# Second layer's experts on one core: row tiles in five buffers in place of three

## The chip, the core and the metric

The kernel runs on one core of a Trainium2 chip. The core has a matrix engine (TensorE; PE in the profile, with its weight loads as PEld), a vector engine (DVE), a scalar engine (ACT), GpSimd (POOL) and a queue engine (SyncE; SP). Sixteen DMA engines move data between the chip's memory and the core's; SP issues most transfers (queue q1), and POOL issues the indirect ones (queue q0). The metric is the device time of one execution in microseconds. Before the change it is 3275.32 us, the median of three runs (3271.12 to 3281.46).

## The reference, cut to what matters

The program is a network of two layers on x of 16 x 512 rows of 256 numbers: a local attention with a feed-forward part, a small routed expert part, a linear attention, and at last a mixture of 8 experts over all 8192 rows, two experts a row. The change touches only this last part:

```python
h = gelu(einsum('ecd,edf->ecf', padded_x, w1), approximate=False)   # D 256 -> F 512
out_padded = einsum('ecf,efd->ecd', h, w2)                          # F 512 -> D 256
out_rep = where(valid[:, None], out_padded[gather_idx], 0.0)
out_w = out_rep * w_topk.reshape(-1)[:, None]
src = src + out_w.reshape(T, TOP_K, D).sum(axis=1)
x = x + gate * rmsnorm(src, norm2_w)
```

## The kernel before, in words

`experts_block` is the last stage of the program. The stage before it has written each row to a list in DRAM (`padded`), sorted by expert; a row there is 260 numbers, the 256 of the row and four more (its destination, and what its weight is made of). The list is cut into 71 tiles (NTILEX) of 256 rows. A tile belongs to one expert, and tile i goes through these steps.

SP loads the rows into `xe` (`load_rows`, L3905 to 3908, 260 KB), and the expert's matrices into `w1` and `w2` (`load_up`, `load_down`, 512 KB each). All three have WB = 3 buffers, and tile i uses buffer i % 3. Destination and expert are numbers that SP reads from a list (`number`, a TENSOR_LOAD of its own for each).

PE transposes the rows (`transpose`, L4116), DVE copies them to `xT` (L4021), PE multiplies with w1 (`up`, L4128), ACT applies gelu (L4011), PE multiplies with w2 (`down`, L4140), and DVE scales the result with the row's weight into `ye` (`copy_out`, L4046). Before that DVE takes destination and weight out of the four extra numbers of the row (`place_rows`, L4030 to 4040). Its first instruction (L4030) waits until the rows sent from the same buffer three tiles ago have arrived.

POOL sends the results with two indirect transfers a tile that add 128 rows each to `src_rows` in DRAM (L3994). Rows of two tiles can have one destination, so the two sends of a tile wait until those of the tile before have arrived. With `ye` and `place` there are three buffers too.

PE's order is transpose(i+2), up(i+1), down(i). DVE's is copy_rows(i+2), place_rows(i), copy_out(i). So place_rows(i) stands behind the transpose of tile i+2, and ahead of copy_out(i) and copy_rows(i+3). In SP's loop step i the rows of tile i+3 are loaded first, once place_rows(i) is over (`weight_ready`), then w1 once up(i) is over, then w2 once down(i) is over. Between them, once in four tiles, stand a load of a gate row, from step 12 on a load of 512 rows of `src_rows` that are complete (L3931), and from step 18 on two stores of the output (L3941). These 512 rows are normalized by DVE and added by POOL (L3982).

After the last tile the last 512 rows are loaded, normalized and stored.

Of the kernel before, what the change touches and what calls it, by code (L numbers as in the profile page):

```python
# [10 lines left out]
ALU = mybir.AluOpType  # L11
AX = mybir.AxisListType

P = 128
D = 256
# [33 lines left out]
ROWS_X = 256  # L49
NTILEX = T * TOPK // ROWS_X + E - 1  # L50

ROW = D + 4
# [3786 lines left out]
def experts_block(nc, m, I, mods_dram, src_dram, padded_dram, out):  # L3839
# [5 lines left out]

    RT = ROWS_X // P
    WB = 3
    ctx = ExitStack()
    with nc.cleanup_on_exit(), ctx:
        def sem(name):  # L3850
# [2 lines left out]
        sb = tile_maker(nc, ctx)  # L3853
        w1 = sb("w1_x", [P, WB, C, F1])
        w2 = sb("w2_x", [P, WB, NF1, D])
        xe = sb("xe", [P, WB, RT, ROW])
        xT = sb("xT_x", [P, 2, C, ROWS_X])
        actT = sb("actT_x", [P, 2, NF1, ROWS_X])
        ye = sb("ye", [P, WB, RT, D])
# [39 lines left out]
        @block.sync  # L3899
        def _(sp):  # L3900
            def number(at, top):
                return nc.values_load(m.tile_x[0:1, at:at + 1], engines=[mybir.EngineType.SP], min_val=0, max_val=top,
                                      skip_runtime_bounds_check_because="the list is clamped to the experts and rows")

            def load_rows(i):  # L3905
                r = number(NTILEX + i, E * CAP)
                sp.dma_start(xe[:, i % WB, :, :], padded_dram[bass.ds(r, ROWS_X), :].rearrange("(t p) d -> p t d", p=P))\
                    .then_inc(x_in[i % WB], 16)

            def load_up(i, e):  # L3910
                sp.dma_start(w1[:, i % WB, :, :], I["L1_ffn_w1"][bass.ds(e, 1), :, :]
                             .rearrange("e (c p) f -> p (e c) f", p=P)).then_inc(w1_in[i % WB], 16)

            def load_down(i, e):
                sp.dma_start(w2[:, i % WB, :, :], I["L1_ffn_w2"][bass.ds(e, 1), :, :]
                             .rearrange("e (f p) d -> p (e f) d", p=P)).then_inc(w2_in[i % WB], 16)

            def rows_sent(n):
                for u in range(WB):
                    sp.wait_ge(sent[u], 16 * RT * ((n + WB - 1 - u) // WB))  # L3920

            def load_gate(b):
                if b:
                    sp.wait_ge(gates_ready, b)
                sp.dma_start(gate_norm[:, b, :], mods_dram[1, b, 2, :].partition_broadcast(P)).then_inc(gates_in, 16)

            def load_src(b):
                rows_sent(complete(b))
                if b >= 2:
                    sp.wait_ge(x_ready, 2 * (b - 1))  # L3930
                sp.dma_start(src[:, b % 2, :, :], src_dram[b * S:(b + 1) * S, :].rearrange("(t p) d -> p t d", p=P))\  # L3931
                    .then_inc(src_in[b % 2], 16)

            def load_last(b, h):
                sp.dma_start(src[:, b % 2, 2 * h:2 * h + 2, :],  # L3935
                             src_dram[b * S + h * (2 * P):b * S + (h + 1) * (2 * P), :].rearrange("(t p) d -> p t d", p=P))\
                    .then_inc(src_in[h], 16)

            def store(b, h):
                sp.wait_ge(x_ready, 2 * b + h + 1)  # L3940
                sp.dma_start(out[b, h * (2 * P):(h + 1) * (2 * P), :].rearrange("(t p) d -> p t d", p=P),  # L3941
                             x_half(b, h).rearrange("p (t d) -> p t d", t=2)).then_inc(stored, 16)

            for i in range(WB):
                load_rows(i)
                e = number(i, E - 1)
                load_up(i, e)
                load_down(i, e)
            sp.dma_start(n2w[:, :], I["L1_ffn_norm2_w"].partition_broadcast(P)).then_inc(gates_in, 16)
            for i in range(NTILEX):  # L3950
                if i + WB < NTILEX:
                    e = number(i + WB, E - 1)
                    sp.wait_ge(xT_done, i + 1)
                    sp.wait_ge(weight_ready, 4 * i + 4)
                    load_rows(i + WB)
                    sp.wait_ge(up_done, 2 * i + 2)
                    load_up(i + WB, e)
                    sp.wait_ge(y_done, i + 1)
                    load_down(i + WB, e)
                if i % 4 == 0:  # L3960
                    if i // 4 < B:
                        load_gate(i // 4)
                    if i >= 12:
                        load_src((i - 12) // 4)
                if i % 4 == 2 and i >= 18:
                    store((i - 18) // 4, 0)
                    store((i - 18) // 4, 1)
            rows_sent(NTILEX)
            sp.wait_ge(x_ready, 2 * (B - 2))  # L3969
            for h in range(2):  # L3970
                load_last(B - 1, h)
            for h in range(2):
                store(B - 2, h)
            for h in range(2):
                store(B - 1, h)
            sp.wait_ge(stored, 16 * 2 * B)
# [38 lines left out]
        def _(dve):  # L4015
# [8 lines left out]
            def place_rows(i):  # L4024
                u = i % WB
                dve.wait_ge(x_in[u], 16 * (i // WB) + 16)

                if i >= WB:
                    dve.wait_ge(sent[u], 16 * RT * (i // WB))
                dve.tensor_copy(place[:, u, :], xe[:, u, :, D]).then_inc(place_ready, 1)  # L4030

                dve.wait_ge(weight_ready, 4 * i)
                dve.scalar_tensor_tensor(out=second[:, :], in0=xe[:, u, :, D + 1], scalar=m.row_x[:, i:i + 1],
                                         in1=m.own[:, :], op0=ALU.subtract, op1=ALU.not_equal).then_inc(weight_ready, 1)
                dve.tensor_tensor(change[:, :], xe[:, u, :, D + 3], xe[:, u, :, D + 2], ALU.subtract)\
                    .then_inc(weight_ready, 1)
                dve.wait_ge(weight_ready, 4 * i + 2)
                dve.tensor_tensor(change[:, :], change[:, :], second[:, :], ALU.mult).then_inc(weight_ready, 1)
                dve.wait_ge(weight_ready, 4 * i + 3)
                dve.tensor_tensor(weight[:, u, :], change[:, :], xe[:, u, :, D + 2], ALU.add).then_inc(weight_ready, 1)  # L4040

            def copy_out(i):
                dve.wait_ge(y_done, i + 1)
# [64 lines left out]
        @block.tensor  # L4108
        def _(pe):
            def transpose(i):  # L4110
                pe.wait_ge(x_in[i % WB], 16 * (i // WB) + 16)
                if i >= 2:
                    pe.wait_ge(xT_ready, i - 1)
                for t in range(RT):
                    for c in range(C):
                        mm = pe.transpose(bank(m, 6 + i % 2)[:, c * ROWS_X + t * P:c * ROWS_X + (t + 1) * P],  # L4116
                                          xe[:, i % WB, t, c * P:(c + 1) * P], m.ident[:, :])
                mm.then_inc(xT_done, 1)

            def up(i):  # L4120
                pe.wait_ge(xT_ready, i + 1)
                pe.wait_ge(w1_in[i % WB], 16 * (i // WB) + 16)
                for h in range(2):
                    if i >= 2:
                        pe.wait_ge(gelu_ready, 2 * (i - 2) + h + 1)
                    for f in (2 * h, 2 * h + 1):
                        for c in range(C):
                            mm = pe.matmul(bank(m, 2 * (i % 2) + h)[:, (f % 2) * ROWS_X:(f % 2 + 1) * ROWS_X],  # L4128
                                           w1[:, i % WB, c, f * P:(f + 1) * P], xT[:, i % 2, c, :],
                                           start=(c == 0), stop=(c == C - 1))  # L4130
                    mm.then_inc(up_done, 1)

            def down(i):
                pe.wait_ge(gelu_ready, 2 * i + 2)
                pe.wait_ge(w2_in[i % WB], 16 * (i // WB) + 16)
                if i >= 2:
                    pe.wait_ge(ye_ready, i - 1)
                for t in range(RT):
                    for f in range(NF1):
                        mm = pe.matmul(bank(m, 4 + i % 2)[:, t * D:(t + 1) * D], actT[:, i % 2, f, t * P:(t + 1) * P],  # L4140
                                       w2[:, i % WB, f, :], start=(f == 0), stop=(f == NF1 - 1))
                mm.then_inc(y_done, 1)

            transpose(0)
            transpose(1)
            up(0)
            for i in range(NTILEX):
                if i + 2 < NTILEX:
                    transpose(i + 2)
                if i + 1 < NTILEX:  # L4150
                    up(i + 1)
                down(i)
# [50 lines left out]
```

## Time and profile before

| | |
|---|---|
| Time before, median of 3 runs | 3275.32 us |
| Profiled execution, its own time | 3295.55 us |
| Span of the profiled execution | 3293.8 us |
| PE busy in the span | 3056.6 us, 93% |
| Last stage | from about 2692 us to the end |
| Transposes of the first and last tile start | 2695.03 and 3251.28 us |

The profiled execution is 20 us longer than the median of the three runs, 0.6%. Durations are read from it, and differences are taken over to the median as they are. Times in the rows are microseconds from the span's start. A busy PE is not a PE at its peak, since matmuls are pipelined and their ends are modelled.

### The profile page before, as it was taken

How to read it: one execution, taken by the hardware profiler on the slowest of the kernel's cores; microseconds unless marked ns; L12 is line 12 of the kernel's file. 1: busy time of each engine (PE TensorE's matmuls, PEld its weight loads, DVE VectorE, ACT ScalarE, POOL GpSimd, SP SyncE). 2: the span in 40 equal slices, each digit the busy share in tenths (PEclk: the TensorE clock that was granted, in tenths of full speed). 3: DMA queues.
4: the chain of work that ended last, by engine and by line, in shares of the span. 5: the costliest groups of instructions: out<-in, count | busy, mean ns of one | idle time of the engine just before them, and what ended most of it. 6: DMA issues, size and time to landing. Idle time of an engine off the chain costs nothing. (4 is left out here: it accounts for less than half of the span.)

```text
span 3293.8 us, 55752 instructions
## 1 busy us (share of the span) xinstructions
PE 3056.6 (93%) x18230; PEld 1911.0 (58%) x18230; DVE 2188.0 (66%) x6629; ACT 1590.7 (48%) x3518; POOL 1202.1 (36%) x1522
## 2 busy tenths in 40 slices
PE   7899999999998995899999999999998859998897
PEld 3566767767765663344444444444443338887786
DVE  7777777777772224778888888888887732445455
ACT  3556565555551113476666666666665521111111
POOL 2123232232244113234444444444443234444445
PEclk9999999999999998899999999999999979999998
DMA  8110010010113971212222222222222128888885
GB/s 271 5 49 25 24 48 24 25 47 24 48 61 116 319 243 44 65 56 74 75 75 75 75 75 75 75 75 75 75 75 72 46 93 218 223 235 222 213 228 148
DMA packets 269343, 337.23 MB, mean 102 GB/s; under 512 B 43951, under 2 KB 218658, under 8 KB 269104
## 3 DMA queue, kind: packets, MB, share of 16 engines
q1 hardware_dynamic: 240112, 296.62, 29.4%
q0 software_dynamic: 28464, 34.71, 4.8%
q10 hardware_dynamic: 544, 3.15, 0.2%
q8 instruction: 113, 1.85, 0.2%
q14 instruction: 110, 0.90, 0.1%
HBM read 225.77 MB, written 113.95 MB: 103 GB/s over the span
## 5 line engine op out<-in xcount | busy, mean ns | idle before, releaser
L2827 DVE TENSOR_REDUCE negmax<-psum 128x1 f32<-128x512 f32 x1024 | 667.0, 683 | 164.6 <-PE psum L3380 149.2
L2445 ACT ACTIVATE pT<-psum 128x512 f32<-128x512 f32 x1024 | 576.0, 595 | 294.2 <-PE psum L3409 200.7
L3380 PE MATMUL psum<-k_stack,q_stack 96*128 96x512 bf16 x1024 | 358.6, 389 | 21.1 <-DVE negmax L2827 16.7
L3409 PE MATMUL psum<-q_stack,k_stack 99*128 99x512 bf16 x1024 | 361.1, 384 | 18.1 <-ACT pT L2445 10.5
L3994 POOL DMA_INDIRECT src_rows<-ye,place x142 | 223.3, 1573 | 330.8 <-DVE place L4030 126.0
L940 ACT ACTIVATE probs<-probs,negmax 128x256 f32<-128x256 f32 x512 | 252.8, 495 | 137.6 <-DVE negmax L1032 133.8
L4011 ACT ACTIVATE actT_x<-psum 128x512 f32<-128x512 f32 x142 | 84.8, 597 | 485.2 <-PE psum L4128 478.5
L3423 PE MATMUL psum<-pT,v_tile 128*32 128x512 f32 x2048 | 269.1, 609 | 1.0 <-ACT pT L2445 1.0
L4128 PE MATMUL psum<-xT_x,w_x 128*128 128x256 f32 x1136 | 263.6, 386 | 0.0
L4140 PE MATMUL psum<-w_x,actT_x 128*128 128x256 f32 x1136 | 256.6, 379 | 0.0
L1032 DVE CUSTOM_DVE_ANT_0 probs<-psum,band_mask 128x256 f32<-128x256 f32 x512 | 181.4, 420 | 104.6 <-PE psum L1296 104.1
L849 POOL TENSOR_TENSOR x<-x,scaled 128x256 f32 (+1 forms) x64 | 46.7, 729 | 552.7 <-DVE scaled L1094 552.7
L4140 PEld LDWEIGHTS psum<-w_x,actT_x 128*128 128x128 f32 x1136 | 215.9, 190 | 29.3
L1354 PE MATMUL psum<-w,actT 128*128 128x256 f32 x1024 | 231.5, 379 | 1.3 <-ACT actT L958 0.8
L4128 PEld LDWEIGHTS psum<-xT_x,w_x 128*128 128x128 f32 x1136 | 215.3, 195 | 27.7
L1348 PE MATMUL psum<-x2T,w 128*128 128x512 f32 x512 | 226.3, 595 | 1.0 <-DVE x2T L1084 1.0
L3380 PEld LDWEIGHTS psum<-k_stack,q_stack 96*128 96x128 bf16 x1024 | 97.3, 98 | 210.6 <-DVE negmax L2827 127.6
L3409 PEld LDWEIGHTS psum<-q_stack,k_stack 99*128 99x128 bf16 x1024 | 99.3, 98 | 201.5 <-ACT pT L2445 109.1
L1354 PEld LDWEIGHTS psum<-w,actT 128*128 128x128 f32 x1024 | 193.4, 190 | 33.7 <-issue 6.2
L4046 DVE TENSOR_SCALAR ye<-psum,weight 128x256 f32<-128x256 f32 x142 | 62.0, 478 | 183.4 <-PE psum L4140 183.0
L1348 PEld LDWEIGHTS psum<-x2T,w 128*128 128x128 f32 x512 | 97.8, 191 | 111.2 <-issue 108.5
L2258 POOL DMA_INDIRECT padded<-src,scatter_idx x128 | 125.6, 981 | 91.3 <-DVE scatter_idx L2973 54.7
(400 smaller groups left out, 5708.9 us busy)
## 6 DMA issues: line engine op xcount, KB each, us to landing
w_x<-in_L_ffn_w_dram SPq DMA_DIRECT2D x142, 512.0 KB, 4.4
w_e<-in_L_ffn_w_dram SPq DMA_DIRECT2D x46, 1024.0 KB, 7.4
q_stacks<-q_part SPq DMA_DIRECT2D x192, 128.0 KB
q_stack<-q_stacks SPq DMA_DIRECT2D x64, 384.0 KB, 4.4
padded<-w_e SPq DMA_DIRECT2D x32, 650.0 KB, 6.1
xe<-padded SPq DMA_DIRECT2D x71, 260.0 KB
gate_rows<-mods SPq DMA_DIRECT2D x66, 256.0 KB, 3.5
x<-in_L_attn_x_dram SPq DMA_DIRECT2D x16, 512.0 KB, 8.7
```

Source lines behind the costliest of these rows:

```text
L940: ins = act.activation(probs[:, h, :], probs[:, h, :], ACT.Exp, bias=negmax[:, h:h + 1], scale=-1.0, accum_out=zsum[:, t % 2, h:h + 1])
L1032: ins = dve.tensor_tensor_reduce(probs[:, h, :], bank(m, j)[:, i * 2 * P:(i + 1) * 2 * P], m.band_mask[:, variant, :], scale=-1.0, scalar= ...
L1348: mm = pe.matmul(bank(m, at), m.w1_0[:, c, f * P:(f + 1) * P], x2T[:, c, :], start=(c == 0), stop=(c == C - 1))
L1354: mm = pe.matmul(bank(m, at)[:, 0:D], actT[:, f, t * P:(t + 1) * P], m.w2_0[:, f, :], start=(f == 0), stop=(f == NF0 - 1))
L2445: act.activation(pT[:, 4 * (s % 2) + r, :], bank(m, 2 + n % 2), ACT.Exp, scale=float(DHQ) ** -0.5)\
L2827: dve.tensor_reduce(negmax[:, p // REP, h:h + 1], bank(m, max_bank(b, 16 * g + p)), AX.X, ALU.max, negate=True).then_inc(max_read, 1)
L3380: pe.matmul(bank(m, max_bank(b, 16 * g + p)), q_stack[0:K_SCORE, h, t * P:(t + 1) * P], k_stack[0:K_SCORE, g, :], start=True, stop=True).t ...
L3409: pe.matmul(bank(m, 2 + n % 2), k_stack[:, g, kc * P:(kc + 1) * P], q_stack[:, REP * g + r, :], start=True, stop=True).then_inc(sT_done, 1)
L3423: mm = pe.matmul(bank(m, VB)[VW * r:VW * (r + 1), :], v_tile[:, par, kc, g, :], pT[:, 4 * (s % 2) + r, :], start=(kc == 0), stop=(kc == NT ...
L3994: pool.indirect_dma_start(src_dram, bass.IndirectOffsetOnAxis(ap=place[:, i % WB, t:t + 1], axis=0), ye[:, i % WB, t, :], None, bounds_che ...
L4128: mm = pe.matmul(bank(m, 2 * (i % 2) + h)[:, (f % 2) * ROWS_X:(f % 2 + 1) * ROWS_X], w1[:, i % WB, c, f * P:(f + 1) * P], xT[:, i % 2, c, ...
L4140: mm = pe.matmul(bank(m, 4 + i % 2)[:, t * D:(t + 1) * D], actT[:, i % 2, f, t * P:(t + 1) * P], w2[:, i % WB, f, :], start=(f == 0), stop ...
```

## The change

The row tiles `xe` get XB = 5 buffers; tile i is in buffer i % 5 everywhere it is read or written. The weights, `ye`, `place` and the semaphores of the loads keep three. The first extra load (tile 3) is issued ahead of the loop, once tile 0 has been transposed. In loop step i SP now loads the rows of tile i+4 in place of those of tile i+3. For that it waits until tile i+1 has been transposed and until place_rows(i-1) is over; before it waited, for tile i+3, until place_rows(i) was over. The load of tile i+4 thus stands one step earlier in SP's order, and what it waits for in DVE's order is two tiles earlier. The loads of w1 and w2 are unchanged, but no wait for place_rows(i) stands ahead of them any more.

```diff
     WB = 3
+    XB = 5
...
-        xe = sb("xe", [P, WB, RT, ROW])
+        xe = sb("xe", [P, XB, RT, ROW])
...
-                sp.dma_start(xe[:, i % WB, :, :], padded_dram[bass.ds(r, ROWS_X), :].rearrange("(t p) d -> p t d", p=P))\
+                sp.dma_start(xe[:, i % XB, :, :], padded_dram[bass.ds(r, ROWS_X), :].rearrange("(t p) d -> p t d", p=P))\
...
             sp.dma_start(n2w[:, :], I["L1_ffn_norm2_w"].partition_broadcast(P)).then_inc(gates_in, 16)
+            sp.wait_ge(xT_done, 1)
+            load_rows(WB)
             for i in range(NTILEX):
+                if i + WB + 1 < NTILEX:
+                    sp.wait_ge(xT_done, i + 2)
+                    if i:
+                        sp.wait_ge(weight_ready, 4 * i)
+                    load_rows(i + WB + 1)
                 if i + WB < NTILEX:
                     e = number(i + WB, E - 1)
-                    sp.wait_ge(xT_done, i + 1)
-                    sp.wait_ge(weight_ready, 4 * i + 4)
-                    load_rows(i + WB)
                     sp.wait_ge(up_done, 2 * i + 2)
                     load_up(i + WB, e)
...
-                dve.tensor_copy(place[:, u, :], xe[:, u, :, D]).then_inc(place_ready, 1)
+                dve.tensor_copy(place[:, u, :], xe[:, i % XB, :, D]).then_inc(place_ready, 1)
```

Three more instructions of place_rows and the transposes get the same new buffer number.

SP's order in the last stage, before, from the last load ahead of the loop to step 1. TENSOR_LOAD reads a number, the DMA on xe loads rows, those on w_x load w1 (128x2x512) and w2 (128x4x256):

```order
L3949 DMA n2w_rows<-in_L_ffn_norm_w_dram 128x256
L3902 TENSOR_LOAD tile_x
L3902 TENSOR_LOAD tile_x [waits d_weight_ready,d_xT_done]
L3907 ISA
L3907 DMA xe<-padded 128x2x260
L3911 ISA [waits d_up_done]
L3911 DMA w_x<-in_L_ffn_w_dram 128x2x512
L3915 DMA w_x<-in_L_ffn_w_dram 128x4x256 [waits d_y_done]
L3925 DMA gate_norm<-mods 128x256
```

The same place after:

```order
L3950 DMA n2w_rows<-in_L_ffn_norm_w_dram 128x256
L3903 TENSOR_LOAD tile_x [waits d_xT_done]
L3908 ISA
L3908 DMA xe<-padded 128x2x260
L3903 TENSOR_LOAD tile_x [waits d_xT_done]
L3908 ISA
L3908 DMA xe<-padded 128x2x260
L3903 TENSOR_LOAD tile_x
L3912 ISA [waits d_up_done]
L3912 DMA w_x<-in_L_ffn_w_dram 128x2x512
L3916 DMA w_x<-in_L_ffn_w_dram 128x4x256 [waits d_y_done]
L3926 DMA gate_norm<-mods 128x256
```

Two row tiles (3 and 4) now stand ahead of the loop's first w1, where there was one, and only transposes hold them. The number of the expert is read behind the rows' load, not ahead of its wait. In later steps the one load of rows in a step is that of a tile further on. The order on PE, DVE, ACT and POOL is the same as before.

## Rows read from the trace of the kernel before

**Rows 1.** Waits in 2692:3294: engine, line, releaser: us in total, times, longest.

```profile
POOL src_rows L3994 <- DMA src_rows<-ye,place: 64.7, 17, 6.4
...
PE psum L4116 <- DMA xe<-padded: 50.6, 25, 12.6
...
DVE place L4030 <- DMA src_rows<-ye,place: 34.8, 24, 5.8
```

**Rows 2.** Waits of the SP queue in 2692:3294.

```profile
SPq L3954 <- DVE weight L4040: 127.7, 53, 8.6
```

**Rows 3.** Transposes of tile 2 and tile 70: start, us, engine, line.

```profile
2706.21 0.60 PE L4116 MATMUL psum<-ident,xe 128*128 128x128 f32 x4
...
3251.28 0.60 PE L4116 MATMUL psum<-ident,xe 128*128 128x128 f32 x4
```

**Rows 4.** Timeline of an early tile, 2750 to 2760.

```profile
2750.29 0.60 PE L4116 MATMUL psum<-ident,xe 128*128 128x128 f32 x4
...
2751.88 0.16 DVE L4030 CAST place<-xe 128x2 uint32<-128x2 f32 x1
...
2753.14 0.37 SPq L3907 DMA_DIRECT2D xe<-padded  x1
...
2757.64 0.60 PE L4116 MATMUL psum<-ident,xe 128*128 128x128 f32 x4
...
2757.84 0.88 DVE L4046 TENSOR_SCALAR ye<-psum,weight 128x256 f32<-128x256 f32 x2 [4.87 <-PE psum L4140]
...
2758.63 0.68 DVE L4021 COPY xT_x<-psum 128x512 f32<-128x512 f32 x1
```

**Rows 5.** Timeline of a late stretch, 3052 to 3080.

```profile
3061.69 1.55 POOL L3994 DMA_INDIRECT src_rows<-ye,place  x1 [0.30 <-issue]
...
3070.41 0.17 DVE L4030 CAST place<-xe 128x2 uint32<-128x2 f32 x1 [5.77 <-DMA src_rows<-ye,place]
...
3071.16 1.55 POOL L3994 DMA_INDIRECT src_rows<-ye,place  x1 [7.91 <-DVE place L4030]
3071.68 0.38 SPq L3907 DMA_DIRECT2D xe<-padded  x1
...
3076.26 1.11 PE L4116 MATMUL psum<-ident,xe 128*128 128x128 f32 x4 [5.44 <-DMA xe<-padded]
```

**Rows 6.** First sends of tiles 1, 11, 31, 62, 67 and 70, POOL's timeline.

```profile
2723.59 1.55 POOL L3994 DMA_INDIRECT src_rows<-ye,place  x1 [4.61 <-PE psum L4128]
...
2796.60 1.55 POOL L3994 DMA_INDIRECT src_rows<-ye,place  x1 [3.70 <-DVE place L4030]
...
2966.30 1.55 POOL L3994 DMA_INDIRECT src_rows<-ye,place  x1 [4.91 <-DVE place L4030]
...
3224.08 1.55 POOL L3994 DMA_INDIRECT src_rows<-ye,place  x1 [4.06 <-DVE place L4030]
...
3257.24 1.55 POOL L3994 DMA_INDIRECT src_rows<-ye,place  x1 [1.99 <-DMA src_rows<-ye,place]
...
3275.50 1.55 POOL L3994 DMA_INDIRECT src_rows<-ye,place  x1 [3.02 <-DMA src_rows<-ye,place]
```

**Rows 7.** Sends (L3994) in 2715:2800, then 2900:3224, then 3224:3294.

```profile
DMA to landing us min/median/max: 4.6/4.9/5.8
...
DMA to landing us min/median/max: 4.1/5.9/8.6
...
DMA to landing us min/median/max: 2.7/3.6/4.9
```

**Rows 8.** Busy time in two stretches, with granted clock, DMA share, GB/s.

```profile
2715.00:2800.00 85.00, 85.00 (x418) 74.83 (x417) 24.59 (x97) 14.33 (x24) 37.17 (x24) 1.00 0.89 219
...
2900.00:3224.00 324.00, 294.41 (x1405) 253.15 (x1404) 162.73 (x577) 46.57 (x78) 145.27 (x95) 0.98 0.84 223
```

**Rows 9.** Scaling of tile 31's result, DVE's timeline.

```profile
2953.78 0.88 DVE L4046 TENSOR_SCALAR ye<-psum,weight 128x256 f32<-128x256 f32 x2 [3.57 <-PE psum L4140]
```

**Rows 10.** PE's waits in 2800:2900, columns as in rows 1.

```profile
PE psum L4116 <- DMA xe<-padded: 5.1, 4, 2.6
```

More of the change, by code:

```diff
@@ L4029, in place_rows @@
                     dve.wait_ge(sent[u], 16 * RT * (i // WB))
-                dve.tensor_copy(place[:, u, :], xe[:, u, :, D]).then_inc(place_ready, 1)
+                dve.tensor_copy(place[:, u, :], xe[:, i % XB, :, D]).then_inc(place_ready, 1)
                 dve.wait_ge(weight_ready, 4 * i)
-                dve.scalar_tensor_tensor(out=second[:, :], in0=xe[:, u, :, D + 1], scalar=m.row_x[:, i:i + 1],
+                dve.scalar_tensor_tensor(out=second[:, :], in0=xe[:, i % XB, :, D + 1], scalar=m.row_x[:, i:i + 1],
                                          in1=m.own[:, :], op0=ALU.subtract, op1=ALU.not_equal).then_inc(weight_ready, 1)
-                dve.tensor_tensor(change[:, :], xe[:, u, :, D + 3], xe[:, u, :, D + 2], ALU.subtract)\
+                dve.tensor_tensor(change[:, :], xe[:, i % XB, :, D + 3], xe[:, i % XB, :, D + 2], ALU.subtract)\
                     .then_inc(weight_ready, 1)
@@ L4039, in place_rows @@
                 dve.wait_ge(weight_ready, 4 * i + 3)
-                dve.tensor_tensor(weight[:, u, :], change[:, :], xe[:, u, :, D + 2], ALU.add).then_inc(weight_ready, 1)
+                dve.tensor_tensor(weight[:, u, :], change[:, :], xe[:, i % XB, :, D + 2], ALU.add).then_inc(weight_ready, 1)
             def copy_out(i):
@@ L4116, in transpose @@
                         mm = pe.transpose(bank(m, 6 + i % 2)[:, c * ROWS_X + t * P:c * ROWS_X + (t + 1) * P],
-                                          xe[:, i % WB, t, c * P:(c + 1) * P], m.ident[:, :])
+                                          xe[:, i % XB, t, c * P:(c + 1) * P], m.ident[:, :])
                 mm.then_inc(xT_done, 1)
```

## The prediction, made before the changed kernel ran

> **What bounds the kernel now.** I read the page first: PE is busy for 93% of the span, so the last stage looks bound by PE too. Then, since the change touches that stage alone, I read the waits from 2692 us to the end, and here the reader is to see that PE waits for one thing only, the rows `xe`: 50.6 us in 25 waits [rows 1]. Two of the 25, 12.6 us for the first tile (the longest) and 3.4 us for the second, are the start of the stage and no part of this. That leaves 34.6 us in 23 waits. The transposes of tiles 2 and 70 start 545.1 us apart, 8.02 us a tile over 68 tiles [rows 3]; undisturbed tiles take 7.35 us [rows 4]. So PE loses 68 x 7.35 = 499.8 against 545.1, 45.3 us, of which 34.6 are waits and some 11 what comes with them (after a wait of 5.44 us four transposes took 1.11 us in place of 0.60 [rows 4, 5]; the granted clock is 0.98 in the late stretch and 1.00 in the early one [rows 8]). 45 us is what a PE that never waits would give back, if nobody else were in the way.
>
> The next view was the SP queue's own waits: it stands 127.7 us in 53 waits ahead of the load of rows, for place_rows [rows 2]. In the early stretch that is harmless. The load leaves 2753.14 and the tile is transposed from 2757.64, 4.5 us later, with no wait [rows 4]. In the late stretch the timeline shows what holds it. place_rows is held up 5.77 us by a send of three tiles ago, until 3070.41; the rows' load leaves 1.27 us behind it, and PE stands until 3076.26 [rows 5]. So the root of PE's wait is the sends. In the waits they stand three more times, with 64.7 us before POOL's next send and 34.8 us before place_rows in 24 waits [rows 1].
>
> Last I followed the sends by themselves, since each pair waits for the landing of the pair before. One cycle is the first send, the second 1.85 us behind it (1.55 and a pause of 0.30 [rows 5]), its landing, and 0.75 us from there to the next first send (3070.41, where the landing also frees place_rows, to 3071.16 [rows 5]). With the median landing of 5.9 us from 2900 to 3224 [rows 7] this makes 1.85 + 5.9 + 0.75 = 8.5 us. Measured, tiles 31 to 62 are (3224.08 - 2966.30) / 31 = 8.32 us apart [rows 6]. In the early stretch it is 1.85 + 4.9 + 0.75 = 7.5 by the medians [rows 7] and (2796.60 - 2723.59) / 10 = 7.30 measured [rows 6], just PE's 7.35. After the last loads it is (3275.50 - 3257.24) / 3 = 6.09 us [rows 6], with landings of 3.6 us [rows 7]. The lag shows who drives. Tile 31's result is being scaled at 2953.78 [rows 9] and is sent at 2966.30 [rows 6], 12.5 us later. The very last pair still starts on a landing, at 3275.50 [rows 6]. So from about tile 24 to the end a chain of sends at 8.3 us a tile sets the pace, and PE's waits for rows are how PE is told to slow down.
>
> **The change part by part.**
>
> The rows' lead. A load issued at 2753.14 for a tile due at 2757.64 is now issued one step of SP earlier, without place_rows(i) ahead: one tile (7.35) and up to the 2.6 us by which it stood behind the end of down, so 12 to 14 us of lead where there were 4.5 [rows 4]. Late, place_rows(i-1) has to be over; even a wait of 5.77 us there [rows 5] leaves more than 4.5 us. PE's 23 waits for rows go: at most -45.3 us for PE. What is late next is place_rows itself, which also stands ahead of copy_out(i) and of the copy for up(i+3) in DVE's order. Undisturbed it starts 1.6 us behind the transpose of tile i+2, and up(i+3) follows the transpose of tile i+4, 14.7 us behind it. After place_rows come its small operations (no more than the 1.26 us from 2751.88 to SP's issue), scaling and copy (0.88 + 0.68, in 1.47 us) [rows 4]. So place_rows may be late by 14.7 - 1.6 - 1.26 - 1.47 = 10.4 us before PE stops, where now 5.77 stop it. PE can be some 5 to 10 us further ahead, about one tile. After that it is again held at the sends' 8.3 us a tile.
>
> What PE's extra tile is worth. The chain of sends does not start earlier for it, as its results wait 12.5 us already [rows 6, 9]. It pays at the end alone: with PE and its loads one tile further ahead, the loads end one tile earlier for the sends, and one to two more tiles are sent at 6.09 in place of 8.32 us: 1.3 x 2.23 = -3 us. Before tile 24, where the chain is caught up with PE, I take another -3 us for PE's first waits, 5.1 us in four, up to 2900 us [rows 10]; its bounds are 0 and -5.
>
> The loads' place in time. The loads of rows and w1 no longer follow a landing by 1.3 us [rows 5] but come at the end of down, next to w2. No row shows sends beside loads in this order. From below: the early stretch has 0.89 of the DMA engines busy and landings of 4.9 us, the late one 0.84 and 5.9 [rows 7, 8], so more load need not mean later landings, and at the early 7.30 us the 31 tiles from 31 to 62 would be 31 x 1.02 = -32 us. From above: landings up to 8.6 us occur [rows 7], and PE runs ahead for some 20 tiles first, with its loads at 7.35 in place of 8.0 us a tile; 0.6 us more on each landing there is +12. I take +2, near the late stretch's rows, which have the full traffic.
>
> The extra row load ahead of the loop, and the two row tiles before the first w1: 260 KB each, with 4.5 us and more until used, beside PE's first transposes; 0, at most +0.5. SP's second number read now stands between rows and w1; w1 has three tiles of lead, 0. The two more buffers cost nothing in time. The end (load, norm and stores after 3277) is unchanged.
>
> Sum against the profiled execution's own 3295.55: -3 - 3 + 2 = -4, so 3291.5; it stands 20 us over the median, so the same difference on 3275.3 gives 3271.
>
> Where a rule would have it otherwise: sends that are issued amid loads land after 5.9 us (median), without them after 3.6 [rows 7], so the loads cost the sends 2.3 us. The Trainium skill, "DMA: Bandwidth & Descriptors", Queues, rings and completion order, says that each DMA engine goes round robin between the queues that have work. By that a send would wait for its share of packets alone, whatever stands behind the load's first ones, and shifting the loads would cost or give nothing: the +2 would be 0, the forecast 3269. The spread from 4.1 to 8.6 us in one stretch [rows 7] speaks against so even a share, and I keep both ends.
>
> **The rivals.**
>
> *The sends follow PE (3230).* If landings only suffer because loads are released by a landing and hit the next pair at once [rows 5], loads spread in time let the chain run at the early 7.30 us, and all of PE's 45 us are won: 3275.3 - 45 = 3230. For it: 7.30 us was held at 0.89 of the DMA engines [rows 6, 8]. Against it: late tiles also load `src_rows` and store, so 7.35 us a tile would need 223 x 8.32 / 7.35 = 252 GB/s where no stretch here has over 223 [rows 8].
>
> *Half of it (3255).* The chain goes at 7.8 in place of 8.32 us over some 38 tiles: -20.
>
> *Slower (3287).* PE, freed, runs its loads ahead at 7.35 us a tile from tile 16 to about tile 36, until place_rows is 10 us late. The sends of these 20 tiles land 0.6 us later each, +12, and are not paid back, as the later pace is the landings' as well. It decides from about 0.5 us a landing on. For it: landings rose from 4.9 to 5.9 with the extra traffic [rows 7]. Against it: the bytes are the same, and what is loaded early isn't loaded late.
>
> *The change doesn't do what it says:* PE still waits for rows, since its lead is eaten by the queue. 12 us of lead against 4.5 speaks against it; the time would be the 3275 of before, within the forecast's range.
>
> **How the numbers follow.** Forecast (the sends keep the pace) 0.54, with its own range 3262 to 3281; half 0.17; all 0.12; slower 0.17. A measurement of this kernel tells about 0.3%, 9.8 us, from no change: faster is under 3265.5, slower over 3285.1. Faster: 0.12 + 0.16 + 0.03 of the forecast's = 0.31; slower: 0.14 + 0.02 = 0.16; within: 0.53. The range leaves out the case at 3230 and half of the slower one, 0.12 + 0.08: 3246 to 3287.
>
> **What would show it.** Right: PE's waits for `xe` fall to the 16 us of the start, and PE waits instead ahead of up (L4128) for the copy to `xT`, or ahead of down for `ye`; place_rows' waits for sends grow well past 34.8 us, single ones to some 10; the lag of sends behind scaling grows from 12.5 to about 20 us; the sends of tiles 31 to 62 stay at 8.2 to 8.5 us. Wrong: sends of the late stretch at 7.3 to 7.8 us (the two faster cases) or landings over 6.5 us in the median (slower), and a lag that does not grow.

## The result

The changed kernel takes 3294.15 us, the median of 5 runs (3293.78 to 3299.34), where before takes 3275.7 (3271.12 to 3281.7): the ratio is 1.0055, with a 95% interval from 1.0039 to 1.007. It is slower by 18 us, outside the forecast range and on the side to which I had given 0.16. Run again later on another chip it was 1.0048 (1.003 to 1.0066).

The profiled execution of the changed kernel took 3294.15 us, span 3292.4. The profiled execution of before, from which all rows ahead of the prediction come, took 3295.55. So the two profiled executions show no loss, where the timed runs show 18 us, and this is the first thing to explain.

What the prediction said of the waits came out. These are the waits of the last stage after, in 2692:3294, columns as in [rows 1]:

```profile
DVE place L4035 <- DMA src_rows<-ye,place: 149.6, 39, 5.8
...
PE psum L4133 <- DVE xT_x L4026: 23.8, 10, 3.5
...
POOL src_rows L3999 <- DMA src_rows<-ye,place: 18.6, 5, 5.4
PE psum L4121 <- DMA xe<-padded: 17.7, 3, 12.7
```

PE's waits for rows fell from 50.6 us to 17.7, the start of the stage and little more. place_rows waits 149.6 us for sends, where it waited 34.8 [rows 1], and PE waits ahead of up (L4133) for the copy to `xT`, which stands behind place_rows.

SP's queue, which had waited 127.7 us for place_rows [rows 2], waits elsewhere:

```profile
SPq L3942 <- POOL x L3987: 92.4, 15, 9.3
SPq L3921 <- DMA src_rows<-ye,place: 25.9, 6, 6.1
SPq L3932 <- DMA src_rows<-ye,place: 25.7, 5, 7.1
SPq L3931 <- DMA src_rows<-ye,place: 25.5, 4, 7.2
```

It comes to the load of `src_rows` (L3921 to 3932) before the sends that it needs have landed, and to the stores (L3942) before POOL's addition (L3987), which stands behind sends in POOL's order. I had not counted these two as waits of SP.

The sends, against [rows 6], in order of time: PE's first transpose with its wait, the scaling of tile 31's result [rows 9], and the first sends of tiles 31, 62 and 70.

```profile
2691.77 1.11 PE L4121 MATMUL psum<-ident,xe 128*128 128x128 f32 x4 [12.68 <-DMA xe<-padded]
...
2947.14 0.87 DVE L4051 TENSOR_SCALAR ye<-psum,weight 128x256 f32<-128x256 f32 x2
...
2962.19 1.55 POOL L3999 DMA_INDIRECT src_rows<-ye,place  x1 [3.11 <-PE psum L4133]
...
3224.00 1.56 POOL L3999 DMA_INDIRECT src_rows<-ye,place  x1 [4.98 <-DVE place L4035]
...
3274.34 1.55 POOL L3999 DMA_INDIRECT src_rows<-ye,place  x1 [1.97 <-DMA src_rows<-ye,place]
```

The lag at tile 31 is 15.1 us (12.5 before), the cycle of tiles 31 to 62 is 261.8 / 31 = 8.45 us (8.32 before), and from the first transpose to the last pair of sends it is 582.6 us; in the profile of before it was 3275.50 - 2695.03 = 580.5. So inside the stage the change is 2.1 us slower even beside that profile. The stage also starts 3.3 us earlier after (2691.77 against 2695.03), in work that the change does not touch.

A stretch of SP, POOL and PE shows the pattern that comes back once in four tiles:

```profile
3038.38 8.70 SPq L3942 DMA_DIRECT2D out_dram<-x  x2
3041.74 1.78 POOL L3999 DMA_INDIRECT src_rows<-ye,place  x1 [6.33 <-DVE place L4035]
...
3047.66 0.39 SPq L3908 DMA_DIRECT2D xe<-padded  x1
3048.47 1.56 POOL L3999 DMA_INDIRECT src_rows<-ye,place  x1 [1.80 <-DVE ye L4051]
3048.85 5.41 PE L4133 MATMUL psum<-xT_x,w_x 128*128 128x256 f32 x16 [3.14 <-DVE xT_x L4026]
...
3049.36 0.41 SPq L3916 DMA_DIRECT2D w_x<-in_L_ffn_w_dram  x1
...
3051.20 0.37 SPq L3912 DMA_DIRECT2D w_x<-in_L_ffn_w_dram  x1
...
3058.33 1.55 POOL L3999 DMA_INDIRECT src_rows<-ye,place  x1 [6.27 <-DVE place L4035]
```

SP stands at the stores until 3047 and then issues five loads in 3.5 us. The pair of sends before the burst takes a cycle of 6.73 us, the pair in it 9.86. PE stops for 3.14 us and then runs up in 5.41 us where it takes 3.62 otherwise: the granted clock from 3048.85 to 3054.26 is 0.68, so for a part of it the clock is at the lower of its two levels, 1.2 GHz.

Two stretches, columns as in [rows 8]:

```profile
2800.00:2900.00 100.00, 100.00 (x491) 88.08 (x490) 52.16 (x187) 16.72 (x28) 43.92 (x29) 1.00 0.89 239
2900.00:3224.00 324.00, 295.85 (x1379) 255.59 (x1378) 159.60 (x566) 45.40 (x76) 146.09 (x95) 0.96 0.81 221
```

First PE never stops and the DMA engines move 239 GB/s. Then all stand behind the sends, the DMA engines are busy for 0.81 of the time (0.84 before) and the granted clock is 0.96 (0.98 before).

### The profile page after: what moved, and what is told of

The parts are those of the page before. It is cut to its first block and busy times, and to the rows that moved or that the text cites. A ratio compares the mean times of both kernels' runs of the same rounds, so it can differ in the third digit from the quotient of the medians.

```text
span 3292.4 us, 55750 instructions
## 1 busy us (share of the span) xinstructions
PE 3059.7 (93%) x18230; PEld 1916.6 (58%) x18230; DVE 2193.8 (67%) x6629; ACT 1591.3 (48%) x3518; POOL 1204.6 (37%) x1522
## 5 line engine op out<-in xcount | busy, mean ns | idle before, releaser
L4133 PE MATMUL psum<-xT_x,w_x 128*128 128x256 f32 x1136 | 271.2, 394 | 27.3 <-DVE xT_x L4026 23.8
L4133 PEld LDWEIGHTS psum<-xT_x,w_x 128*128 128x128 f32 x1136 | 219.5, 198 | 59.9 <-DVE xT_x L4026 26.1
L1306 PE MATMUL psum<-ident,probs 128*128 128x128 f32 x1024 | 133.5, 282 | 24.7 <-ACT probs L940 24.6
```

## The experiments

Each is one edit of the kernel before or after, timed beside the kernel before on the same chip. Chips differ (the median of before was 3265.8 us on one and 3282.9 on another), so the ratios are what compares.

**Before again, and the buffers alone.** The first has no edit. The second is the changed kernel with before's loop in SP:

```diff
-            sp.wait_ge(xT_done, 1)
-            load_rows(WB)
...
-                if i + WB + 1 < NTILEX:
...
-                    load_rows(i + WB + 1)
                 if i + WB < NTILEX:
                     e = number(i + WB, E - 1)
+                    sp.wait_ge(xT_done, i + 1)
+                    sp.wait_ge(weight_ready, 4 * i + 4)
+                    load_rows(i + WB)
```

> The kernel before, unchanged, to get a second profile. The profiled execution of before took 3295.6 us, 20 us over its own timed runs, and that of the changed kernel 3294.2, just its median. Theory A (before has two patterns in the last stage, and the first profile caught the slow one): a time of 3271 to 3282 and a profile whose last stage is 10 to 20 us shorter than 602 us, with send cycles of tiles 31 to 62 near 8.0 us in place of 8.32. Theory B (the profile itself costs before 15 to 20 us): a profiled span near 3294 again while the timed runs stay at 3271 to 3282.

> Five buffers for the row tiles as in the changed kernel, but their loads issued where and when the kernel before issues them. If the order of the loads makes the changed kernel slower (my theory), this is at the time of before, 3271 to 3282 us. If the place of the buffers in memory does (rival), it is at 3290 to 3296.

Measured: before again 1.0009 (0.9992 to 1.0027), 12 runs from 3276.6 to 3303.9 us; the buffers alone 0.9989 (0.9974 to 1.0003). The 29 runs of before in this comparison went from 3272.5 to 3294.7 us. The profiled execution of before again took 3290.5 us, that of the buffers alone 3280.2. From the latter, again the first transpose, then the first sends of tiles 31 and 70:

```profile
2696.68 1.11 PE L4117 MATMUL psum<-ident,xe 128*128 128x128 f32 x4 [12.63 <-DMA xe<-padded]
...
2956.84 1.55 POOL L3995 DMA_INDIRECT src_rows<-ye,place  x1 [4.51 <-DMA src_rows<-ye,place]
...
3260.13 1.55 POOL L3995 DMA_INDIRECT src_rows<-ye,place  x1 [2.97 <-DMA src_rows<-ye,place]
```

From the first transpose to the last sends it is 563.5 us, 19.1 less than after, close to the 18 us of the timed runs. In before again it is 575.0. What is left of the three executions with before's order of loads is nearly equal (3295.55 - 580.5 = 2715.1, 3290.5 - 575.0 = 2715.5, 3280.2 - 563.5 = 2716.7), so their differences lie in this stage. The lag at tile 31 is 4.2 us in the buffers alone (2952.62 to 2956.84), 4.3 in before again, 12.5 in the first profile; at tile 52 it is 10.7, 10.8 and 11.9.

So with before's order of loads an execution can run either way: with the sends close behind their results for half of the stage, or for all but its start far behind them, and then it takes as long as the changed kernel. The first profile had caught the latter. Theory B is out, since the profiled execution of the buffers alone lies at its own median. Theory A holds in kind and not in its figures: before again was only 5.5 us shorter than the first profile, with a cycle of 8.29 us for tiles 31 to 62 where I expected 8.0 (8.13 in the buffers alone), and the times spread in place of forming two groups. The buffers' place costs nothing.

The waits of before again hold one thing more:

```profile
PE psum L4116 <- DMA xe<-padded: 46.6, 26, 12.6
...
DVE place L4030 <- DMA src_rows<-ye,place: 2.0, 4, 0.7
```

place_rows hardly waits for sends here, and PE waits for rows nearly as long as in the first profile.

**Half of the sends.** In both kernels each tile is sent with its first transfer alone:

```diff
-                for t in range(RT):
+                for t in range(1):
```

(and all counts of `sent` halved, so half of the rows are never added to `src_rows`).

> The kernel before with only the first of the two sends of each tile, so half of the rows are never added to the result. If the chain of sends sets the pace of the last stage (my theory), its cycle falls from 1.85 + 5.9 + 0.75 to about 0 + 6 + 0.75, under PE's 7.35 us, PE's waits for rows go, and the time falls by about 40 us to 3235. If PE's waits come from the loads' short lead as such (rival), it stays within 10 us of 3275.

> The changed kernel with only the first of the two sends of each tile, half of the rows not added. By my theory it falls to the same 3235 us as the kernel before with one send, within 5 us, since neither is then held by sends. If the changed order of loads costs time by itself (rival: more load on the DMA engines), it stays 15 to 20 us above that one.

Measured: before with half of the sends 0.9963 (0.9947 to 0.9978), the changed kernel with half of them 0.9878 (0.985 to 0.9906): 3268.4 and 3243.6 us. For the kernel before, the 40 us that the chain of sends promised did not come. It stayed 7 us under 3275, as the rival had it (10.9 under before on its own chip, at the rival's edge). For the changed kernel both theories missed: it is neither equal to the other nor 15 to 20 us above it, but 25 us below. In the kernel before PE goes on waiting for rows, and after it doesn't; the waits of the last stage of the two, before first, with two more lines of before:

```profile
PE psum L4116 <- DMA xe<-padded: 35.3, 27, 12.7
...
SPq L3954 <- DVE weight L4040: 99.5, 49, 7.3
...
L4030 DVE CAST place<-xe x71: 156/159/1992, 2703.0 to 3242.7; 128x2 uint32<-128x2 f32 x71
its engine sat idle before it (us, times) until:
who waited for it (us, times):
  POOL src_rows L3994: 343.1, 57
```

```profile
PE psum L4121 <- DMA xe<-padded: 17.6, 2, 12.7
...
2900.00:3224.00 324.00, 324.00 (x1585) 285.40 (x1584) 154.88 (x652) 52.55 (x88) 98.62 (x67) 1.00 0.77 227
```

With half of the sends no send in the kernel before starts more than 2.4 us behind its result, and place_rows never waits for one (nothing stands under "sat idle"). SP still waits 99.5 us for place_rows, which stands behind the transpose of tile i+2 in DVE's order, and PE still takes 7.84 us a tile in tiles 31 to 62. Of the 34.6 us behind the start of the stage in the first profile (50.6 less the first two waits) 19 us are left here. So more than half of PE's waits for rows are the short lead's own, and not the sends'.

And the sends do hold the changed kernel: with half of them it is 1.2% under before, PE is busy for 324.00 of 324 us, and the same change is worth 25 us. The change does what it says; it is the full load of sends that turns it round.

**Which part does it.** Four kernels, on one chip. The stores of the changed kernel four steps later (the two that the loop then no longer reaches stand behind it); SP's wait for place_rows(i) put back ahead of w1; both; and the rows of tile i+3, not i+4, loaded in step i, without the wait for place_rows(i):

```diff
-                if i % 4 == 2 and i >= 18:
-                    store((i - 18) // 4, 0)
+                if i % 4 == 2 and i >= 22:
+                    store((i - 22) // 4, 0)
```

```diff
                     e = number(i + WB, E - 1)
+                    sp.wait_ge(weight_ready, 4 * i + 4)
                     sp.wait_ge(up_done, 2 * i + 2)
```

```diff
                 if i + WB < NTILEX:
                     e = number(i + WB, E - 1)
+                    sp.wait_ge(xT_done, i + 1)
+                    if i > 1:
+                        sp.wait_ge(weight_ready, 4 * i - 4)
+                    load_rows(i + WB)
```

> The changed kernel with the two stores of a group issued four steps of SP later (22 in place of 18), so that SP finds their sums ready. In the changed kernel SP stood 92.4 us in 15 waits at these stores and then issued two tiles' loads at once. If these bursts are what makes the sends late (theory: bursts), the stores' wait goes, the alternation of landings of about 4.6 and 8.5 us evens out, and the time falls by 8 to 18 us from 3294. If it is only that PE and its loads run ahead of the sends (rival: ahead), the wait moves to the load of src_rows, and the time stays within 5 us of 3294.

> The changed kernel with one wait put back: ahead of the load of w1 SP waits for place_rows(i) again, so rows still go early, but each of SP's steps is paced by the sends as before. Bursts: SP no longer gets to the stores early, and the time is that of before or up to 10 us under it, 3268 to 3280. Ahead: PE's limit is then w1's lead of nearly three tiles, PE is still a tile further ahead than before, and the time stays over 3285.

> Both edits of the two kernels before this one. If bursts are the cause and both remove them, it is at the time of the better one within 4 us. If it is faster than before by over 5 us, the change's longer lead is worth something once SP's pace is kept.

> Five buffers, and the rows of tile i+3 loaded in step i as in the kernel before, but without the wait for place_rows(i) (it waits for place_rows(i-2), which has long been over). It takes from the change only the step in SP's order. If the freed pace does the harm, not the step, it is slow like the changed kernel, 3288 to 3298. If the step does it (two row tiles in a burst with w1), it is at 3272 to 3284.

Measured: stores later 1.0045 (1.0029 to 1.0061); w1 paced 1.0107 (1.009 to 1.0123); both 1.0147 (1.0128 to 1.0165); no step 0.9991 (0.9981 to 1.0002). The wait at the stores is not the cause: without it the time is that of the changed kernel, and SP now waits 66.4 us for place_rows ahead of the rows. The wait for place_rows put back ahead of w1 makes it worse, by about 0.5% alone and by 1% with the stores later, where I had expected the better time of the two. So my theory of bursts failed. The wait for place_rows ahead of the rows, taken away alone, does no harm: the one step in SP's order does it. That was one of the two cases that I had named for the last kernel, though for another reason (a burst of two row tiles with w1). The kernel without the step from 2900 to 3224, and a piece of its timeline:

```profile
2900.00:3224.00 324.00, 309.14 (x1502) 268.08 (x1501) 146.50 (x599) 50.04 (x84) 156.49 (x104) 1.00 0.86 234
```

```profile
3043.09 0.38 SPq L3908 DMA_DIRECT2D xe<-padded  x1
3043.59 1.56 POOL L3996 DMA_INDIRECT src_rows<-ye,place  x1 [1.87 <-PE psum L4130]
...
3049.74 0.66 PE L4118 MATMUL psum<-ident,xe 128*128 128x128 f32 x4 [1.79 <-DMA xe<-padded]
...
3053.27 1.56 POOL L3996 DMA_INDIRECT src_rows<-ye,place  x1 [4.97 <-DMA src_rows<-ye,place]
```

Its rows are loaded 5.4 to 6.0 us before their transpose in tiles 6 to 13, and 6.65 us in the lines shown, the wait included (another load, of `src_rows`, stands ahead of them here); the change has 13.0 to 13.6 in tiles 6 to 13. PE still pauses for them, 1.79 us here and 20.5 us in 19 waits behind the start of the stage, none over 2.0. The sends stay 2 to 5 us behind their results to the end, place_rows never waits for them, and the DMA engines move 234 GB/s in place of 221. Short and long cycles alternate here as well: in tiles 31 to 62 they are 6.6 and 9.1 us in the mean, 6.5 and 10.2 in the changed kernel. So the alternation is not what the change brought, only the longer long cycle.

**Holding PE by the sends, and a lead between.** The changed kernel again; with PE's transpose of tile i waiting for the sends of tile i-4, or of i-5; and with the load of rows between w1 and w2:

```diff
                 pe.wait_ge(x_in[i % WB], 16 * (i // WB) + 16)
+                if i >= 4:
+                    pe.wait_ge(sent[(i - 4) % WB], 16 * RT * ((i - 4) // WB + 1))
```

```diff
                     load_up(i + WB, e)
+                    if i + WB + 1 < NTILEX:
+                        sp.wait_ge(up_done, 2 * i + 4)
+                        if i:
+                            sp.wait_ge(weight_ready, 4 * i)
+                        load_rows(i + WB + 1)
                     sp.wait_ge(y_done, i + 1)
```

> The changed kernel unchanged, as the anchor for the three beside it: 18 to 20 us (0.55%) over before on this chip, too, with sends 12 us or more behind their results at tile 45.

> The changed kernel with a wait added on PE: the transpose of tile i starts only when the sends of tile i-4 have landed. Theory (back-pressure): PE's short waits for rows in before kept PE at the sends' heels, and near their results sends land sooner; the change took these waits away, the sends fell 12 us and more behind, and each cycle got longer. Then this added wait brings the lag at tile 45 back to 2 to 5 us, the send cycle of tiles 31 to 62 from 8.4 to 7.8 to 8.1 us, and the time back to before or under it (0.996 to 1.001 of before). Rival (the place of the loads in the queue does the harm, not the lag): the lag goes but the time stays 0.4% or more over before, or gets worse by the added waits.

> As the kernel before this one, but PE waits for the sends of tile i-5, one tile looser. Back-pressure: the lag is held at 6 to 10 us, and the time lies between the two, 1.000 to 1.004 of before. Rival: as the changed kernel, 1.005.

> The changed kernel with the load of the rows of tile i+4 put between those of w1 and w2, once up(i+1) is over, which makes its lead about 10.5 us, between the 6 us of the kernel without the step (0.999 of before) and the changed kernel's 13 to 14 (1.0055). Back-pressure: rows are hardly ever late at 10 us either, the sends fall behind, and the time is 1.003 to 1.006 of before. Rival (two row tiles and w1 issued together do it): the loads are now spread over the step, and the time is at 0.997 to 1.001.

Measured, in this order: 1.0048 (1.003 to 1.0066), 1.0246 (1.0226 to 1.0266), 1.0061 (1.0041 to 1.0081), 1.006 (1.0041 to 1.0079). The changed kernel again had the expected lag, 12.7 us at tile 45. With the wait for tile i-4 the lag there was 2.7 us, as expected, and the time the worst of all: PE waits 84.9 us in 36 waits, and the DMA engines are 0.76 busy and move 200 GB/s.

```profile
2900.00:3224.00 324.00, 270.75 (x1238) 231.81 (x1239) 125.18 (x512) 40.80 (x69) 128.36 (x85) 0.95 0.76 200
```

With tile i-5 the lag at tile 45 was 8.5 us, as expected, and PE waited 35.7 us in 28 waits, but the time did not come down. So a small lag by itself does not make the stage fast, and the test missed. It can't tell back-pressure from its rival either, since PE's own waits are so long in it. The lead between (9.8 to 10.2 us in tiles 6 to 13) was as slow as the longest, as back-pressure has it; spreading the loads did not help.

**Holding PE by the loads.** What was open is whether PE's pauses for late rows matter, or the earlier load's place in SP's queue. So the changed kernel, SP untouched, with PE's transpose of tile i waiting for the rows of tile i+1 too; the same with down(i) waiting for the rows of tile i+3; and no step again:

```diff
                 pe.wait_ge(x_in[i % WB], 16 * (i // WB) + 16)
+                if 3 <= i < NTILEX - 1:
+                    pe.wait_ge(x_in[(i + 1) % WB], 16 * ((i + 1) // WB) + 16)
```

```diff
             def down(i):
+                if 1 <= i < NTILEX - 3:
+                    pe.wait_ge(x_in[(i + 3) % WB], 16 * ((i + 3) // WB) + 16)
```

> The changed kernel with one wait added on PE: the transpose of tile i also waits for the rows of tile i+1. Nothing in SP's order changes. The rows that PE waits for then have a lead of 13.7 - 7.35, some 6.3 us, like those of the kernel without the step (0.999 of before). Back-pressure by the loads: PE again pauses a microsecond or two when the DMA queue is backed up, the sends stay 2 to 4 us behind their results up to tile 31, their cycle is 7.8 to 8.1 us, and the time is 0.996 to 1.001 of before. Rival (it is the place of the earlier row load in SP's queue): 1.004 to 1.007, as the changed kernel.

> The same wait set later: down(i) waits for the rows of tile i+3, whose lead there is about 10 us. Back-pressure: at 10 us it hardly ever holds PE, as in the kernel with the rows' load between w1 and w2 (1.006), so 1.003 to 1.007 of before. Rival (any wait of PE for loads helps): under 1.001.

> The kernel without the step again, beside the two others: 0.997 to 1.001 of before, with PE waits for rows of about 20 us after the start. If it comes out over 1.003, its first result was one chip's chance, and the step is not what does the harm.

Measured: 0.9971 (0.9953 to 0.9989), 1.0033 (1.0017 to 1.0049), 0.9977 (0.9961 to 0.9993). The first turns the changed kernel's loss into a gain with nothing but a wait added to PE: 3260.3 us beside 3270.4 of before. The kernel without the step gains as much on this chip; on the other it was level with before. The waits of the first kernel and its late stretch:

```profile
PE psum L4123 <- issue: 19.7, 18, 2.1
```

```profile
2900.00:3220.00 320.00, 306.25 (x1488) 265.83 (x1487) 145.34 (x599) 49.27 (x83) 156.80 (x104) 1.00 0.86 234
```

(The profile puts this wait down to "issue", since the transpose's own rows had long landed.) PE pauses 19.7 us in 18 waits of at most 2.1, and the stage runs like that of the kernel without the step. With the looser wait the sends fall back as in the changed kernel (11.9 us at tile 20, where the first has 1.7), and place_rows waits for them again:

```profile
DVE place L4035 <- DMA src_rows<-ye,place: 153.1, 39, 6.8
...
PE psum L4147 <- DMA xe<-padded: 16.7, 8, 3.7
```

PE waits nearly as long in total for rows here, 16.7 us, but in eight waits of which the first comes at 2919, when the sends have long fallen back. So it is not the sum of PE's pauses that counts. No run slowed PE by a fixed amount, so whether the pauses have to follow the loads is not shown.

## Why the prediction was wrong, point by point

*The first views.* That PE waits for rows alone, and that the sends form a chain with a cycle of about 8.3 us, were right for the execution that was profiled. "So the root of PE's wait is the sends" was read off one tile and does not hold in general: in before again place_rows waits 2.0 us for sends and PE 46.6 us for rows, and with half of the sends PE still waits 35.3. Of the sends' waits I wrote that they stand "three more times", and named two.

*The change part by part* was right as to who waits: PE's waits for rows went, place_rows and the copy behind it became the limit, with single waits to 5.8 us (I had expected some 10), and the lag grew, from 12.5 to 15.1 us at tile 31 (I had expected about 20). Later the lag was no larger than before (12.9 and 13.3 us at tile 45). Sum against the profiled execution's own time: -4 us forecast, 3294.15 - 3295.55 = -1.4 measured, but +2.1 within the stage. By parts, from the first sends against [rows 6]: tiles 1 to 31 -0.2 (forecast -3), tiles 31 to 62 +4.0 (forecast +2), tiles 62 to 70 -1.1 (forecast -3). So PE's first waits gave nothing, and the end a third.

*The step that failed* is the one behind that sum: "it stands 20 us over the median, so the same difference on 3275.3 gives 3271". The 20 us were no cost spread over the whole, but the very thing under study. They were the lagging sends, which the profiled execution had from tile 24 on: its stage took 580.5 us, that of the buffers alone, in an execution at its own median, 563.5. The two later profiles with before's order of loads have them for the second half of the stage only; that most timed runs do as well is inferred from their times. The sentence "from about tile 24 to the end a chain of sends at 8.3 us a tile sets the pace" was true of that execution and not of the kernel. The change has the slow pattern in both of its profiles, from tile 20 on, and its five runs lie within 0.2%, at the time of that profile.

*What PE's waits are worth* I had as at most a gain. I wrote that they are how PE is told to slow down, and drew nothing from it. My reading now: the loads are issued by PE's progress, so each short pause for late rows holds back loads and lets the sends catch up. That a wait for rows alone restores the stage is shown by the kernel with the next tile's rows; the draining in between is argued. In the changed kernel PE stays at 7.35 us a tile from tile 2 to tile 30 without a pause (in the buffers alone a pause comes every second to fourth tile from tile 16 on), the sends fall behind, and once the buffers of `ye` and `place` are full, place_rows, SP's load of `src_rows` and its stores all wait, and the DMA engines are busy for 0.81 of the time in place of 0.86. Against the buffers alone the pairs of tiles 13 to 31 come 8.44 us apart in place of 7.89, and those of 31 to 62 8.45 in place of 8.13: 18 x 0.55 + 31 x 0.32 = 9.9 + 9.9 = 20 us, about the 19.1 between the two stages.

*The rivals.* Slower was the right side, for a mechanism near the real one (PE's loads ahead of the sends). Its price, 0.6 us on 20 tiles and 12 in all, was right for those tiles; that the later ones cost as much again was not in it, as I took 8.32 us for their pace in before. Its sign came early and went: the median landing rose from 6.3 to 6.8 us in 2800:2900, but fell from 5.9 to 4.8 from 2900 to 3224, where short and long cycles alternate. The faster cases failed: sends at 7.3 us a tile were reached by no kernel with all of them, and the best, at 0.9971, has 7.7 to 7.9. Against them I had held that no stretch of before moves over 223 GB/s; from 2800 to 2900 it moves 227, and after it is 239. That moving the loads would cost the sends nothing failed as well.

*What stays open.* Why, with the same bytes, the sends take 8.4 us a tile far behind their results and 7.8 close behind them (where PE itself takes 7.8) is shown only as the DMA engines' share (0.81 against 0.86) and the waits that go with it. It was not shown that the lag by itself lengthens a landing, and the kernels in which PE waits for sends speak against the lag alone.

## What to carry to other kernels

A wait of the busiest engine for a load is not always a loss to be bought off with buffers. Where loads share the DMA engines with a serial chain of transfers, it can be what keeps the loads from running over the chain; before lengthening a lead, ask what the freed engine will overrun, and keep a wait that bounds it, as the transpose's wait for the next tile's rows does here. A wait seen behind a chain of transfers in one tile is not yet caused by it: take the transfers away, as half of the sends did here, and see whether the wait goes. And where the profiled execution lies outside the timed runs, the difference is not a constant to be subtracted: first find which stage it is in.

## What was not expected of the hardware

The same program on one core gave 3272.5 to 3294.7 us in 29 runs on one chip, 0.7%, while the changed kernel's first five runs spread by 0.2%, and six on another chip by 0.3%. Three profiles with before's order of loads differ by 17.0 us from the first transpose to the last sends (580.5, 575.0 and 563.5), and by under 2 us in all the rest; what makes one execution fall back earlier than another was not found. A wait added to PE for data that it did not yet need made the kernel 0.8% faster (1.0048 to 0.9971, two chips); the same kind of wait for sends in place of loads made it 2% slower.
